# Recurrence stage of a decoder layer: bias pieces ahead of the high-down pieces, and quarters of regrouped rows issued ahead of the wait for stored rows

## What is computed

```python
x = x + recurrence(layernorm(x))           # 4 steps in t, state of 64, 8 blocks
x = x + cross_attention(layernorm(x), ctx) # 16 heads of 32
h = layernorm(x) @ W_exp + b_exp           # 512 -> 2048
h = butterfly(h, up_weights)               # 11 stages, pairs i and i ^ 2**stage
h = gelu(h + up_bias)
h = butterfly(h, down_weights)             # 11 stages
x = x + h @ W_con + b_con + down_bias      # 2048 -> 512
```

## Time and profile before

| | us |
|---|---|
| median of 3 runs | 2265.24 (2263.72 to 2268.49) |
| the profiled execution | 2265.3, of which its span is 2263.5 |
| PE busy | 2218.5 (98%) |
| recurrence, groups 4 to 8 | 87.37 to 161.18 |
| transfers of the SP queue | 440.72 MB, 60.2% of 16 engines' span |

### The profile page before, as it was taken

One profiled execution on the slowest core, in us unless ns is written; L12 is line 12 of the kernel. 1 busy time (PEld: TensorE's weight loads), 2 busy tenths in 40 slices (PEclk: granted clock), 3 DMA queues, 4 the chain that ended last, 5 costly groups with the idle time before them and its releaser, 6 DMA issues.

```text
span 2263.5 us, 41277 instructions
## 1 busy us (share of the span) xinstructions
PE 2218.5 (98%) x15960; PEld 1943.2 (86%) x15960; DVE 1701.5 (75%) x2854; ACT 1231.5 (54%) x2735; POOL 467.4 (21%) x578
## 2 busy tenths in 40 slices
PE   8899889999999999999999999999999999999999
PEld 7678777888888888778989989989989989889899
DVE  6666688888888888857947858758769668579467
ACT  3556566666766666645535536446446356355343
POOL 3531222322223222300020200300300300300203
PEclk8999999999999999999999999999999999999999
DMA  9999613323332331466676686786676676766765
GB/s 319 329 320 319 226 66 122 124 86 112 109 110 86 117 124 62 146 238 206 212 263 184 215 269 174 220 268 195 204 267 208 211 245 207 240 214 209 229 188 194
DMA packets 202091, 443.35 MB, mean 196 GB/s; under 512 B 32442, under 2 KB 70586, under 8 KB 200362
## 3 DMA queue, kind: packets, MB, share of 16 engines
q1 hardware_dynamic: 201898, 440.72, 60.2%
HBM read 341.66 MB, written 99.01 MB: 195 GB/s over the span
## 4 chain that ended last, share of the span: by engine, by line
PE 87%; ACT 5%; DVE 5%; DMA 2%; issue 1%; SPq 0%; POOL 0%; DVEq 0%; POOLq 0%; ACTq 0%
PE ps L442 69%; PE ps L1989 5%; PE ps L1957 4%; PE ps L1968 2%; ACT es L1085 2%; DMA yg<-in_wcon 1%; PE ps L1920 1%; PE ps L1877 1%; ACT wc_h L1041 1%; PE ps L1808 1%; DMA x_scratch<-xa 1%; PE ps L1859 1%; DVE rsum L1492 1%; ACT es L1090 1%; PE ps L1872 1%
## 5 line engine op out<-in xcount | busy, mean ns | idle before, releaser
L442 PE MATMUL ps<-ring,gh 128*128 128x256 f32 x3584 | 652.8, 284 | 0.1
L442 PEld LDWEIGHTS ps<-ring,gh 128*128 128x128 f32 x3584 | 558.2, 192 | 2.1 <-DVE gl L1314 1.5
L442 PE MATMUL ps<-xth,ring 128*128 128x512 f32 x1792 | 553.1, 389 | 0.0
L442 PE MATMUL ps<-ring,gl 128*128 128x256 f32 x1792 | 506.8, 283 | 0.0
L442 PEld LDWEIGHTS ps<-xth,ring 128*128 128x128 f32 x1792 | 336.4, 188 | 69.7
L1182 ACT ACTIVATE gh<-G 128x512 fp32r<-128x512 f32 x384 | 239.2, 629 | 218.6 <-PE ps L442 218.2
L442 PE MATMUL ps<-xtl,ring 128*128 128x512 f32 x896 | 348.6, 389 | 0.0
L442 PEld LDWEIGHTS ps<-ring,gl 128*128 128x128 f32 x1792 | 343.5, 192 | 0.0
L1314 DVE TENSOR_TENSOR gl<-G,gh 128x512 fp32r<-128x512 f32 x384 | 276.5, 732 | 51.4 <-ACT gh L1182 50.3
L866 POOL TENSOR_TENSOR es<-es,rinv 128x308 f32<-128x308 f32 x256 | 180.5, 736 | 388.8 <-DVE rinv L1496 388.8
L1165 ACT ACTIVATE G<-G,up_b 128x512 f32<-128x512 f32 x192 | 138.9, 723 | 222.0 <-DVE G L1608 222.0
(11 more groups left out here) (234 smaller groups left out, 4394.0 us busy)
## 6 DMA issues: line engine op xcount, KB each, us to landing
ring<-wup_scratch SPq DMA_DIRECT2D x224, 512.0 KB, 3.8
ring<-wdn_scratch SPq DMA_DIRECT2D x224, 512.0 KB, 3.6
X<-x_scratch SPq DMA_DIRECT2D x32, 1024.0 KB, 9.0
xa<-in_x SPq DMA_DIRECT2D x16, 1024.0 KB, 6.6
x_scratch<-xa SPq DMA_DIRECT2D x16, 1024.0 KB, 10.6
x<-x_scratch SPq DMA_DIRECT2D x16, 1024.0 KB, 5.6
x_scratch<-x SPq DMA_DIRECT2D x16, 1024.0 KB, 4.3
out_x<-X SPq DMA_DIRECT2D x15, 1024.0 KB, 6.4
```

What stands on the lines that cost most here:

```text
L442: mm = pe.matmul(bank, a, b, start=first and i == 0, stop=last and i == n - 1, skip_group_check=go_on)
```

## The change

Two edits, both in the recurrence stage. First, the numbers of the pieces: the four bias pieces BL become 16 to 19, and the sixteen high-down pieces DH become 20 to 35; all conditions on these numbers follow. The wait ahead of the yd quarters is now for 36 stored pieces, where it was 32, and the load of `bg` is issued at piece 23 instead of 39. Second, `quarter(g)` is called after the pieces of chunk 0, ahead of the `stored` wait and the load of x, where it was called after both in chunk 1. No instruction is added or removed; line numbers above L587 are one higher behind the edit.

```diff
-        LU, DH, BL, UH, BH, DL = 0, MC, 2 * MC, 2 * MC + 4, 3 * MC + 4, 3 * MC + 8
+        LU, BL, DH, UH, BH, DL = 0, MC, MC + 4, 2 * MC + 4, 3 * MC + 4, 3 * MC + 8
...
             def bias_rows(n):
-                if n == UH + 3:
-                    staged(UH)
+                if n == DH + 3:
+                    staged(DH)
                     sp.dma_start(bg[:, :], b_d[0].rearrange("a (q j) -> (a q) j", j=MC)).then_inc(bg_loaded, 16)
...
                 if XG_AT <= g < XG_AT + 4:
                     q = g - XG_AT
-                    staged(DH)
+                    staged(BL)
...
                 if YD_AT <= g < YD_AT + 4:
                     q = g - YD_AT
-                    staged(BL)
+                    staged(UH)
                     sp.wait_ge(piece_pe, UH + 4 * q + 4)
...
                     if g == 2 and c == 0:
                         store_v()
+                    if c == 0:
+                        quarter(g)
                     if c == 1:
                         if g:
                             stored(sp, x1_stored, g - 1)
                         if g and g + 4 < NG:
                             load_x(g + 4)
-                        quarter(g)
...
                 if g == 11:
-                    sp.wait_ge(piece_pe, BL)
+                    sp.wait_ge(piece_pe, UH)
```

More of the change, by code:

```diff
@@ L535, in piece_out @@
                 src, out = stage[n % STAGES], stage_out[n % STAGES]
-                if n < DH:
+                if n < BL:
                     sp.dma_start(wl_d[P * (n - LU):P * (n - LU + 1)], src[:, :]).then_inc(out, 16)
-                elif n < BL:
+                elif n < DH:
+                    sp.dma_start(b_d[0][n - BL:n - BL + 1], src[0:1, :]).then_inc(out, 16)
+                elif n < UH:
                     sp.dma_start(wh_d.rearrange("(p j) n -> j p n", j=MC)[n - DH], src[:, :]).then_inc(out, 16)
-                elif n < UH:
-                    sp.dma_start(b_d[0][n - BL:n - BL + 1], src[0:1, :]).then_inc(out, 16)
                 elif n < BH:
@@ L978, in piece_back @@
                 after(act, stage_out[n % STAGES], 16 * (n // STAGES))
-                rows = 1 if BL <= n < UH or BH <= n < DL else P
+                rows = 1 if BL <= n < DH or BH <= n < DL else P
                 ins = A(stage[n % STAGES][0:rows, :], bank[0:rows], ACT.Copy)
@@ L1837, in piece @@
                     mm = pe.matmul(bank, tup[:, c * P:(c + 1) * P], xu[:, c, :], start=True, stop=True)
-                elif n < BL:
+                elif n < DH:
+                    if n == BL:
+                        pe.wait_ge(bias_loaded, 32)
+                    for i in range(4):
+                        c = 4 * (n - BL) + i
+                        mm = pe.matmul(bank[0:1, i * P:(i + 1) * P], be[:, c:c + 1], tup[:, c * P:(c + 1) * P], start=True, stop=True)
+                elif n < UH:
                     j = n - DH
@@ L1844, in piece @@
                     mm = pe.matmul(bank, mq[1][:, j, :], yg[:, j, :], start=True, stop=True)
[L1845 to L1850, removed]
                 elif n < BH:
```

## The result

The changed kernel takes 2254.45 us (median of 6 runs, 2253.19 to 2256.17) against 2265.39 us beside it: 10.9 us less by the medians. The ratio is 0.9948, 95% interval 0.9938 to 0.9959, which is 11.8 us (9.3 to 14.0). The forecast was 2253.0, 12.3 us less.

The account below looks back on a forecast made before the run. PE is busy 98%, so only its waits and low clock can be won: 15.32 us excess in groups 4 to 8, less 1.6 that stays, less 1.4 for late transfers, gives 12.3; 2265.3 becomes 2253.0 us, range 2249.8 to 2259.0.

Parts of the forecast that it names:

- The waits for yg and the clock: Recurrence groups 4 to 8: all four PE waits for yg, 9.4 us, go, and with them the low clock.
- What stays of the excess: Groups 4 and 7: DVE's msum meets GpSimd's mq_dn or mq_up; 0.8 us stays in each, 1.6 of 15.32.
- the double price: Group 7: the DVE and GpSimd collision costs double, lowering the gross gain from 13.7 to 12.9 us.
- the tie: Group 7: msum and mq_up start nearly together, either may be blocked; without a collision the gross gain is 14.5 us.
- The transfers: Loads of x, groups 4 to 11: seven loops move 31.2 MB at 0.36 MB/us in 86.7 us.
- the 1.4 us of lateness: Group 13: the last load of x lands at 198.7 us against a limit of 197.3, costing 1.4 us.
- Edit 1 alone is worth little: Recurrence: moving only the bias pieces ahead gains little for long, since SP's loop is slower than PE's.
- Behind the stage the gain stays: Attention and feed-forward after the recurrence are PE-bound with DMA shares of 1 to 8 tenths, so the gain stays.
- The transfers hold it: Rival, chance 0.11: loads of x or piece stores come late in groups 9 to 13; 2257 to 2260 us.
- The quarter moves nothing: Rival, chance 0.07: PE's own pieces or the transfer rate hold yg, the stall returns; within 4.5 us of before.
- Slower, the quarter takes the store's bandwidth: Rival, chance 0.05: stores of rows land up to 2.9 us later in each loop; 2281 us at full price.
- The signs that were named: Groups 4 to 8 in 59 to 61 us, quarters landing after 10 to 13, DMA share 0.95 or more in groups 6 to 12.

Follow-up runs that it names:

- the run with the matrices later: Changed kernel with the last step of mq_dn and mq_up on GpSimd one iteration later; ratio 0.9956 to the kernel before.
- Edit 1 alone: Changed kernel with quarter(g) back behind the wait for stored rows and the load of x, bias pieces still ahead; ratio 1.0001 to the kernel before.
- ubs late: Changed kernel with the load of ubs moved from group 13 to behind group 14's row store; ratio 0.9937, rerun 0.9947, to the kernel before.
- edit 2 alone: Kernel before with only quarter(g) moved ahead of the wait for stored rows, pieces in their old order; ratio 0.9959, 9.3 us gained.

## Why the prediction was right, point by point

**The waits for yg and the clock.** All four waits went, groups 5 and 7 run at 1.00. Right. The quarters were issued at 80.68, 94.98, 104.99 and 118.38 us and landed at 92.7, 106.2, 116.0 and 129.0; forecast were 81, 94, 106, 119 and 92, 106, 117, 131.

**What stays of the excess.** Forecast 0.8 us each in groups 4 and 7, measured 0.98 and 1.57 (12.51 and 13.10 less 11.53). Of the 0.98, about 0.2 is the bias piece that now stands in group 4 (three of them make group 5 0.56 longer than 11.53), so that term was right. The one in group 7 was at the double price that the prediction had as its bound, and it was mis-sized by 0.8 us. Groups 4 to 8 gained 13.0 us where 13.7 was forecast. DVE then GpSimd in group 7 of the changed kernel:

```profile
126.58 0.15 DVE L1290 TENSOR_TENSOR msum<-st 128x4 f32<-128x4 f32 x1
...
126.72 3.73 DVE L1292 TENSOR_TENSOR sq<-st 128x4 f32<-128x4 f32 x1
...
126.65 3.79 POOL L769 TENSOR_TENSOR mq_up<-path_up,same 128x2048 f32<-128x2048 f32 x1
```

It was the tie that the prediction saw: msum and the one behind it went through in 0.15 and 0.16 us, and sq, which started 0.07 us after mq_up on GpSimd, was held for 3.73 us, longer than msum in group 4, 2.90. That the second to start is held agrees with the Trainium skill, SBUF — State Buffer, Who interferes with whom. That the collision caused the excess is shown by the run with the matrices later.

**The transfers.** Forecast 86.7 us for the seven loops, measured 86.79; the last load of x issued at 188.47 (forecast 189.2), landed at 196.7 (198.7), its limit 197.3. So the 1.4 us of lateness did not come: DVE waited 1.2 us at the longest, and PE not at all in groups 9 to 13. The issue to landing was 8.2 us, not 9.5; I had added the whole quarter ahead of it, of which a part was probably through, which no row shows. The rate of 0.36 MB/us that the prediction chose was right for the seven loops as a whole, though single groups moved 294 to 401 GB/s. By the estimate from the 425 GB/s that the Trainium skill gives for a 16 MB load (DMA: Bandwidth & Descriptors, Bandwidth) the loops would not bind; here they did, and moved 360 GB/s at a share of 1.00.

**Edit 1 alone is worth little.** Right, 1.0001. On top of edit 2 it takes the ratio from 0.9959 to 0.9948, 2.5 us; the intervals overlap, so this part rests on the trace alone (the wait of 4.2 us in group 6 that it covers).

**Behind the stage the gain stays.** Wrong by 1.4 us in the profiled execution (1.38 us between group 14 and the scores; 0.44 in the second one of the changed kernel, 42.34). The load of x1 rows landed at 224.3, statistics waited for it, and in group 15 a piece waited for a stage:

```profile
226.32 2.04 PE L1873 MATMUL ps<-yd,wgd 128*128 128x512 f32 x2 [2.96 <-ACT stage L981]
...
224.36 2.47 DVE L1278 BATCH_NORM_STATS2 st<-x 128x6 f32<-128x512 f32 x4 [3.40 <-DMA x<-x_scratch]
```

The prediction had followed the lead of the loads of x to group 13 and stopped there; the same lead is wanted once more by the first load of x1 rows in group 14. That these two waits are the 1.4 us is not shown: with ubs late both were nearly gone, and the stretch was 43.09 us all the same. So the forecast gain of 12.3 less 0.7 (collision), plus 1.4 (lateness that did not come), less 1.4 (tail) is 11.6; the traces show 13.03 - 1.38 = 11.65 from group 2 to the scores. That the last two terms cancel is luck.

**The rivals.** "The transfers hold it": the changed kernel stands at the limit but not behind it; every further gain fell to this rival. "The quarter moves nothing": out, by the run with edit 2 alone. "Slower, the quarter takes the store's bandwidth": stores landed after 8.5 to 14.2 us, 10.4 in the median (8.3 to 12.1 and 10.6 in the earlier trace rows); out for the loops as a whole. One store did show it: that of 75.20, with the first quarter issued behind it, took 14.2 us, where the one of 76.66 took 11.59 before.

**The signs that were named.** Groups 4 to 8 took 60.79 us, group 9 began at 147.46, group 13 at 194.81, and the quarters landed after 10.6 to 12.0 us, all as named. The DMA share of group 6 was 0.83 and not 0.95 or more; from group 7 to 12 it was 0.98 to 1.05. Of the signs of being wrong one came: two stores took 14.2 us (13 was the limit named), one ahead of the seven loops and one behind them, at 233.04. The stores in between took 8.8 to 12.3.

**What the prediction had right by a wrong reading.** It took the late quarters for the cause and the loop for a limit that comes after. The runs show the order reversed. With the quarters of yg in time and the loop still 13.8 us long, nothing was gained. So the loop, with engines that ran dry for 8% of it, was what cost time, and yg the first place where PE met it. The sum came out because, by this reading, the idle time at yg and the dry time of the seven loops were the same debt: 13.0 us from group 2 to group 14, of which 8.1 are the shorter loops (94.92 against 86.79) and 4.8 are lead that PE has used up: SP issued the load of x in group 11 12.82 us after the group began (197.38 and 184.56), and now 17.65 us after (188.47 and 170.82).

## What to carry to other kernels

If a sequencer waits for a transfer to land before it issues the next, put what is ready behind that transfer into the queue before the wait: what counted here is that the DMA engines had work while SP waited, not when that piece of work was needed. A wait of the compute engine for a certain tile tells where a debt falls due, not where it was made: sum bytes and DMA share over whole loops before believing it, and test with a run in which that tile comes in time by another way. Once the loops are bound by transfers and the lead is used up, what shortens PE's work only moves its wait (the run with the matrices later). A share of 1.00 does not give the rate: loops at 1.00 and 1.01 moved 360 and 375 GB/s here.

## What the runs showed that was not expected

- A load of 8 KB in 2048 elements of 4 bytes makes the next DMA that SP issues take 7.76 us (7.28 in the second execution), if it follows at once; with the load of ubs moved away it took 0.36. In the kernel before the next issue came 3.4 us behind it and took 3.67 (a yd quarter at 221.23). No cost of it was seen in this kernel's time.
- Removing 2.3 us of held DVE time in groups 4 and 7 came back as 4.4 us in groups 10 and 11 of one execution. Executions of the same kernel also differ in where they wait: in the two profiled ones of the changed kernel, DVE waited 2.4 and 4.8 us for loads of x, 3.4 and 1.6 for the first x1 rows, and the spans are 2.4 us apart.
